# Ten of sixteen attention iterations written as a loop of five rounds instead of straight-line code

## What is computed

```python
x = x + jnp.tanh(g_xattn[0]) * xattn(layernorm(x), ctx, Wq, Wk, Wv, Wo, bo)
x = x + jnp.tanh(g_ffn[0]) * ffn(layernorm(x), router_w, w_gate, w_up, w_down, ...)

def xattn(x, context, Wq, Wk, Wv, Wo, bo):
    ...
    scores = jnp.einsum('bhqd,bhkd->bhqk', q, k) * SCALE
    scores = jnp.where(causal[None, None, :, :], scores, -jnp.inf)
    probs = jax.nn.softmax(scores, axis=-1)
    y = jnp.einsum('bhqk,bhkd->bhqd', probs, v)
    y = y.transpose(0, 2, 1, 3).reshape(b, t, c)
    return y @ Wo.T + bo
```

## Time and profile before

| | us |
|---|---|
| median of 3 runs | 2062.74 (2062.62 to 2062.76) |
| the profiled execution, its own time | 2062.74 |
| its span, from the first to the last instruction | 2061.0 |
| busy: PE / DVE / ACT / POOL | 2017.0 / 1147.9 / 793.4 / 191.6 |

### The profile page before, as it was taken

One profiled execution on the slowest core, in us unless ns is written; L12 is line 12 of the kernel. 1 busy time (PEld: TensorE's weight loads), 2 busy tenths in 40 slices (PEclk: granted clock), 3 DMA queues, 4 the chain that ended last, 5 costly groups with the idle time before them and its releaser, 6 DMA issues.

```text
span 2061.0 us, 32955 instructions
## 1 busy us (share of the span) xinstructions
PE 2017.0 (98%) x12160; PEld 1684.6 (82%) x12160; DVE 1147.9 (56%) x2766; ACT 793.4 (38%) x1974; POOL 191.6 (9%) x395
## 2 busy tenths in 40 slices
PE   6999999999997999999999999999999999999999
PEld 6899999999985778888888888777888888888887
DVE  6888888898887744333433343465334333333333
ACT  4777777777775522111111111243111111111111
POOL 3221221322212100000000000010000000000000
PEclk9999999999998999999999999999999999999999
DMA  7555655655643201000000010131001000100002
GB/s 210 136 132 139 149 128 143 148 129 144 142 104 126 82 21 31 21 21 21 31 20 20 20 31 21 62 103 41 21 21 31 21 21 20 31 31 20 10 1 82
DMA packets 117508, 138.36 MB, mean 67 GB/s; under 512 B 9728, under 2 KB 91648, under 8 KB 117376
## 3 DMA queue, kind: packets, MB, share of 16 engines
q1 hardware_dynamic: 117376, 136.63, 24.7%
HBM read 69.49 MB, written 16.78 MB: 42 GB/s over the span
## 4 chain that ended last, share of the span: by engine, by line
PE 63%; DMA 1%; DVE 1%; ACT 1%; POOL 1%; issue 1%; SPq 0%; POOLq 0%; DVEq 0%; ACTq 0%
PE gate_up L1181 41%; PE down L1200 21%; DMA acc<-x_between 1%; ACT xn L919 1%; DVE norm_stats L890 1%; DMA out<-acc 0%; PE gate_up L1158 0%; POOL norm_newton L97 0%; DVE xt_lo L1049 0%; PE down L1145 0%; PE gate_up L1165 0%; POOL norm_rstd L97 0%; ACT L1016 0%; POOL norm_newton L95 0%; DVE h L1088 0%
## 5 line engine op out<-in xcount | busy, mean ns | idle before, releaser
L1181 PE MATMUL gate_up<-xt_hi,e_hi 128*128 128x512 f32 x1280 | 507.3, 396 | 0.0
L1181 PE MATMUL gate_up<-xt_hi,e_lo 128*128 128x512 f32 x1280 | 506.4, 396 | 0.0
L1181 PE MATMUL gate_up<-xt_lo,e_hi 128*128 128x512 f32 x1280 | 506.3, 396 | 0.0
L1088 DVE TENSOR_TENSOR h<-gate_up,silu 128x512 f32<-128x512 f32 x160 | 110.5, 691 | 558.1 <-PE gate_up L1181 545.9
L1016 ACT ACTIVATE silu<-gate_up 128x512 f32<-128x512 f32 x160 | 95.7, 598 | 565.3 <-PE gate_up L1181 565.2
L1102 DVE SCALAR_TENSOR_TENSOR acc<-down,scale,acc 128x512 f32<-128x512 f32 x320 | 238.1, 748 | 109.3 <-PE down L1200 107.1
L1181 PEld LDWEIGHTS gate_up<-xt_lo,e_hi 128*128 128x128 f32 x1280 | 240.4, 188 | 58.3
L1181 PEld LDWEIGHTS gate_up<-xt_hi,e_hi 128*128 128x128 f32 x1280 | 240.5, 188 | 58.0
L1181 PEld LDWEIGHTS gate_up<-xt_hi,e_lo 128*128 128x128 f32 x1280 | 240.5, 188 | 57.6
L1019 ACT CAST h_hi<-h 128x512 fp32r<-128x512 f32 x160 | 99.4, 621 | 456.1 <-DVE h L1088 456.1
L1200 PE MATMUL down<-e_hi,h_hi 128*128 128x512 f32 x640 | 253.3, 396 | 0.9 <-DVE acc L1102 0.9
(11 more groups left out here) (129 smaller groups left out, 3300.6 us busy)
## 6 DMA issues: line engine op xcount, KB each, us to landing
k_stack<-k_hi SPq DMA_DIRECT2D x128, 128.0 KB, 2.6
q_stack<-q_hi SPq DMA_DIRECT2D x128, 128.0 KB, 2.6
w_raw<-in_w_gate SPq DMA_DIRECT2D x20, 512.0 KB, 3.7
w_raw<-in_w_up SPq DMA_DIRECT2D x20, 512.0 KB, 3.8
w_raw<-in_w_down SPq DMA_DIRECT2D x20, 512.0 KB, 3.6
c_in<-in_ctx_t SPq DMA_DIRECT2D x16, 512.0 KB, 3.6
x_in<-in_x SPq DMA_DIRECT2D x16, 512.0 KB, 3.8
k_stack<-k_lo SPq DMA_DIRECT2D x64, 128.0 KB, 2.6
```

Source lines behind the costliest of these rows:

```text
L1088: dve.tensor_tensor(h[f][:], gu_ps[f][:, 1, :], silu[f][:], ALU.mult).then_inc(h_made, 1)
L1181: ins = pe.matmul(gu_ps[f][:, which, :], (hi, lo)[a][:, c, f * P:(f + 1) * P], (xt_hi, xt_lo)[b][:, blk, c, :], start=(i == 0), stop=(i == ...
```

## The change

It replaces the unrolled list of attention iterations by 4 straight iterations (-1 to 2), a loop of 5 rounds with 2 iterations in each (3 to 12), and 4 straight iterations (13 to 16), on each of the five engines. Two iterations per round keep the parity of the double buffers fixed within the loop's code. The work, the order of instructions within an iteration, the buffers and the semaphores stay as they are; inside the loop the counted values of waits and the sequence numbers of the DMAs become register expressions.

```diff
+    FIRST, PAIRS = 3, 5
+
     def iterations(eng, run):
 
-        for i in range(-1, B + 1):
+
+
+        for i in range(-1, FIRST):
+            run(At(0, 2, i))
+        with eng.Fori(0, PAIRS) as r:
+            for u in range(2):
+                run(At(r, 2, FIRST + u))
+        for i in range(FIRST + 2 * PAIRS, B + 1):
             run(At(0, 2, i))
```

## The result

| | median, us | |
|---|---|---|
| before | 2062.75 | (2062.62 to 2064.26) |
| after | 2098.31 | (2096.86 to 2099.81) |

The change makes the kernel slower: the ratio is 1.0175, 95% interval 1.0161 to 1.019, or 35.6 us more. The forecast was 2067.3, with a range of 2062.7 to 2075.5. The sign was right and the size was not.

What follows compares the result with a forecast made beforehand. The prediction took PE to bound the kernel, with DVE following. To 2062.7 us it added 1.0 for register work, 0 for the branch and 3.6 for code at the loop's head, giving 2067.3, range 2062.7 to 2075.5.

Steps and rivals of the forecast that it cites:

- What bounds the kernel: Whole kernel: PE busy 2017.0 of 2061.0 us sets the pace; DVE follows with 4.3 us to spare per iteration.
- (2) The branch: Four branches back and one fall-through on each engine: no time lost for the branch itself.
- (1) Register work: Register instructions for waits and DMA addresses in ten iterations: 0.1 us each, 1.0 us in all, bounds 0 to 3.
- (3) Code at the loop's head: At four branches back, DVE's bare fetch of the head delays PE 0.9 us each: 3.6 us, bounds 0 to 10.8.
- The fetch's price: One code fetch at a branch back: 2.5 us taken, from a range of 2.1 to 3.3 us.
- The lead: DVE's sequencer ahead of its engine at the branch back: 1.2 us of queued work, covering part of the fetch.
- rival C: Bare fetch at branches back: DVE has no lead or waits two fetches, 5.0 us; about 2075 us; chance 0.20.
- The forecast's own term: One DVE fetch at each branch back, mostly covered: DVE 1.3 us late, PE stands 0.9 us.
- rival A: All loop code stays in the engines, so the change does next to nothing: 2063.7 us; chance 0.33.
- What the profile after would show: Signs: later-round code packets and DVE or PE gaps of one to three us starting iterations 5, 7, 9, 11.
- D (waits that grow): Register work delays more steps in every looped iteration, 0.5 us in each of ten: 2067.7 us; chance 0.07.
- E (faster): Register instructions carry waits that are separate now, gaining under 0.1 us an iteration, 1 us in all; chance 0.04.

Runs made afterwards that it cites:

- one fetch was left alone: Changed kernel with PE's and ACT's loop heads at a code block's border and DVE's at instruction 64 of a block: 2071.37 us, ratio 1.0037.
- the aligned loop: Changed kernel with the loop heads of PE, DVE and ACT each put at a code block's border: 2064.87 us, ratio 1.0004.
- the layout with a first stall of 2.6 us and a short second one: Changed kernel with PE's loop head put at instruction 200 of a code block: 2087.1 us, ratio 1.0118.

## Why the prediction was wrong

**What bounds the kernel** was right: PE, with DVE behind it. **(2) The branch** costs nothing: with all heads at a border no iteration of the loop is longer at its border.

**(1) Register work.** Forecast 1.0 us, bounds 0 to 3; measured 0.1 us over nine iterations, or at most 0.05 us in each of ten, 0.5 us. Only the size was off.

**(3) Code at the loop's head** names the right cause and the right iterations, and then fails at one sentence: "ACT's own fetch runs at the same time as DVE's, and so does PE's, at a moment when PE's sequencer has to wait at the new iteration's first scores for DVE's maxima anyway; I add nothing for them." The wait is real, but it covers next to nothing. The first scores need the maxima of two heads back, and in before these are done at 305.07, 1.0 us before the scores start at 306.08:

```profile
304.99 0.08 DVE L550 DVE_READ_ACCUMULATOR2_ANT neg_max<- 128x1 f32 x1
```

PE's sequencer runs ahead of the array, so its wait ends while the array still has work, and the array never stands there. A fetch that lasts longer than that queued work is bare. What PE's code costs at a branch is a first fetch, 2.6 to 2.9 us of the array, a second fetch, 3.4 to 4.3 us, and about 2.5 us of the half clock that goes with the two stalls: 8.9 us where the forecast has nothing, times four.

The fetch's price of 2.5 us was too low, as the sequencers' own records show, which the listings leave out. In the kernel with only DVE looped, DVE's branch starts at 231.91 and the first work behind it at 235.14: 3.2 us, near the forecast's upper bound of 3.3. The lead was right: the residual of 232.38 ends at 233.11, 1.2 us after the branch. On PE the branch alone lasts 4.25 us in after (229.88 to 234.13) and 0.2 in the experts' loop, and the array had 1.9 us queued. The packet itself is in transfer for only 1.0 of these 4.25 us. The text's way, a landing of 2.1 to 2.6 us and a packet of 1.2, would give 3.3 to 3.8 for PE; it took 2.1 to 3.3 for both engines. The second fetch, from the branch's end to 237.98, lasts 3.85 us with a single matmul queued. That is why the second stall is the longer one.

The second fetch was in the text, in rival C ("a fetch into a full store pushes out the next one that is needed"), but for DVE only. There two fetches and the size are right: 3.4 us at a branch on average with DVE alone in a loop, where C had 2.7 to 3.4. The forecast's own term, one fetch at 0.9 us, measured 1.6 where one fetch was left alone: DVE is 2.0 us late, not 1.3. PE meets this at the rows' low part and not at the keys'. In before that low part ends at 311.18 and the projection that waits for it starts at 311.91, a cushion of 0.7 and not 0.4, and 2.0 - 0.7 = 1.3; with one fetch PE's projection starts 1.4 us late. The other 0.2 us of the 1.6 are not accounted for.

**Whether the code stays.** The text had "No row shows a body of that size kept" and set the border for rival A at "PE keeps about 6.5 packets". The body of 6.4 is in fact kept, if it lies well. The length alone doesn't decide; the blocks that it touches and the one fetched ahead do, and the forecast counted only the length, without register instructions (6.2 and 2.5 packets for 6.4 and 2.7).

Of the Trainium skill's page Advanced Engine Details and Errata, section ISA Cache, the sizes fit what the runs show: 128 KB is eight packets of 16 KB, 32 KB four of 8 KB, and seven plus one on PE and three plus one on DVE stay, while one more doesn't. The two cache lines that this page of the Trainium skill also states don't fit: with aligned heads no code is fetched in four rounds. The Trainium skill's page Runtime: NRT & Kernel Launch, section Instruction fetch mechanics, says that kernels prefer to be unrolled; after agrees by 35.6 us, the aligned loop by nothing that can be measured.

**What the profile after would show.** Right: code packets in the later rounds, and loss at iterations 5, 7, 9 and 11 alone. The sentence "The prediction is wrong if [...] time is lost only on PE's own fetch" is what came about. D (waits that grow) and E (faster) are excluded by the 38.18 us iterations. The range failed because it held nothing for the engine that sets the pace, with its own clock behind it. Nor did it hold all of DVE's worst case: four times 3.4 and (1) is 2077.3, above the 2075.5 at which the range ends, and DVE alone in a loop measured 2077.27.

**What stays open:** what fills the 3 us of a fetch in which its packet is not in transfer, and whether the data transfers beside it (63% and 76% of the DMA engines' time in the windows of the two packets) lengthen it; the 6 us at the exit with three hints; and the last 1 to 2 us between the aligned loop and the kernel before, which the measurement hardly resolves. That eight and four blocks are kept is inferred from which layouts fetch; that the clock's fall comes from the stalls was not tried by itself, it only goes with them: with DVE's loss alone, one shorter stall for each branch, it fell in one of four, for 3.4 us.

## What to carry to other kernels

Before rolling a loop, count its body on each engine in blocks of code, register instructions and waits included, and add the blocks that the ends cut and the one that is fetched ahead. If that exceeds what the engine keeps (here eight blocks of 16 KB on PE, four of 8 KB on DVE), move the head to a border before giving up. Cost the fetch first on the engine that sets the pace: there it is bare, and a second one follows if the head lies just before a border. A cost that was hidden behind a larger one shows up when that is removed, so mend all engines together (35.6 us became 14 with PE alone aligned and 1 with three).

## What the runs showed of the hardware

- A block's fetch holds PE's array for 2.6 to 2.9 us, with 1.9 us of work queued ahead of it, though its packet is in transfer for only 4.6% of 16 x 1.4 us = 1.0 us.
- In after, two idle times of PE, of 2.4 to 2.7 and 3.2 to 4.0 us with one matmul between, go with 6.8 us at the half clock at all four branches, beginning at the first of them 1.7 us before the second idle time ends. In the layout with a first stall of 2.6 us and a short second one the clock was lower as well (0.56 in 234.0 to 240.8):

```profile
234.00:240.80 6.80, 5.89 (x39) 5.71 (x38) 3.54 (x12) 2.72 (x10) 0.00 (x0) 0.56 0.24 84
```

- A branch hint removes the fetches of the loop. On PE alone it costs nothing at the exit (38.17 us for the first iteration behind the loop); on PE, DVE and ACT together that iteration takes 6 us more.
- The code fetched ahead takes a place: a body that touches eight blocks on PE has nine packets in each round, and one that touches seven has none.
